# Written-out head groups without work for missing neighbours, and output additions ahead of the pair's second low part

## What is computed

```
# layer 0 (perceiver attention: keys of context and of the latents, RMS-normed q and k)
q  = rmsnorm(ln(x) @ Wq) * scale ;  k, v = split(concat(ln_x(ctx), ln(x)) @ Wkv) ; k = rmsnorm(k)
x += tanh(g) * (softmax(q @ k.T) @ v @ Wout + bout)
# layer 1 (keys of context and one null key)
x += tanh(g) * ln(softmax(q * scale @ k.T) @ v @ Wo)
```

## Time and profile before

| | |
|---|---|
| median of 3 runs | 4423.91 us (4422.67 to 4423.99) |
| the profiled execution | 4427.17 us |
| its span, first to last instruction | 4425.4 us |
| mean granted TensorE clock | 0.974 |
| TensorE busy | 4081.1 us, 92% |
| VectorE busy | 3433.7 us, 78% |
| ScalarE busy | 3199.6 us, 72% |
| GpSimd busy | 408.8 us, 9% |
| low parts, L824 | 1764 of 1223 ns |
| first attention layer | some 116 to 2294 us |
| second attention layer | some 2516 to 4367 us |

### The profile page before, as it was taken

The page is one execution under the profiler, slowest core; times in us unless marked ns, Lnnn a source line. Parts: engine busy times, 40 slices in busy tenths (PEclk is TensorE's granted clock), DMA queues, the critical chain, the costliest instruction groups (busy, mean ns, idle before and its releaser), DMA issues. The chain is left out here.

```text
span 4425.4 us, 74954 instructions
## 1 busy us (share of the span) xinstructions
PE 4081.1 (92%) x25901; PEld 2675.9 (60%) x26341; DVE 3433.7 (78%) x5288; ACT 3199.6 (72%) x5181; POOL 408.8 (9%) x348
## 2 busy tenths in 40 slices
PE   3999999999999999999978599999999999999995
PEld 2666666666666666666656366666666666666663
DVE  5888788787887878888867577777777777777775
ACT  3888888888878888888853367676766676666662
POOL 3111111111111111111110000000000000000000
PEclk9999999999999999999978699999999999999997
DMA  1000000000000000000003000000000000000001
GB/s 41 13 1 16 1 5 13 1 16 1 17 1 1 16 1 16 1 1 16 1 24 102 17 1 16 1 14 3 5 12 5 13 1 16 1 16 1 16 1 42
DMA packets 31247, 54.26 MB, mean 12 GB/s; under 512 B 9856, under 2 KB 19080, under 8 KB 28552
## 3 DMA queue, kind: packets, MB, share of 16 engines
q1 hardware_dynamic: 28808, 48.66, 3.5%
q10 hardware_dynamic: 2066, 0.69, 0.1%
HBM read 48.44 MB, written 0.88 MB: 11 GB/s over the span
## 5 line engine op out<-in xcount | busy, mean ns | idle before, releaser
L824 DVE TENSOR_TENSOR a_probs_lo<-a_probs 128x1024 fp32r<-128x1024 f32 x1764 | 2119.9, 1223 | 649.7 <-ACT a_probs L669 305.7
L665 ACT ACTIVATE a_probs<-scores_ps,a_c_bias,a_k_rstd 128x512 f32<-128x512 f32 x1892 | 1315.8, 775 | 31.6 <-PE scores_ps L1141 30.1
L1166 PE MATMUL out_ps<-a_probs_lo,a_v 128*128 128x512 f32 x3520 | 1135.6, 443 | 0.0
L1159 PE MATMUL out_ps<-a_probs,a_v 128*128 128x512 bf16 x3080 | 858.9, 390 | 113.6 <-issue 51.0
L669 ACT ACTIVATE a_probs<-scores_ps,a_c_bias 128x1024 f32<-128x1024 f32 x818 | 869.7, 1111 | 111.6 <-PE scores_ps L1141 110.7
L1141 PE MATMUL scores_ps<-a_q_hi,a_k_hi 64*128 64x512 f32 x3528 | 793.3, 445 | 11.0 <-ACT a_probs L665 6.3
L1166 PEld LDWEIGHTS out_ps<-a_probs_lo,a_v 128*128 128x128 f32 x3520 | 659.6, 188 | 220.8 <-issue 0.6
L1141 PE MATMUL scores_ps<-a_q_lo,a_k_hi 64*128 64x512 f32 x3528 | 702.8, 393 | 0.0
L1141 PE MATMUL scores_ps<-a_q_hi,a_k_lo 64*128 64x512 f32 x3528 | 698.4, 391 | 0.0
L1159 PEld LDWEIGHTS out_ps<-a_probs,a_v 128*128 128x128 f16 x3520 | 273.9, 97 | 592.8 <-issue 222.4
L634 ACT ACTIVATE a_v<-proj_ps 128x256 f16<-128x256 f32 x456 | 175.0, 384 | 520.7 <-PE proj_ps L1076 520.7
(11 more groups left out here) (233 smaller groups left out, 3455.8 us busy)
## 6 DMA issues: line engine op xcount, KB each, us to landing
a_den<-a_inv_row SPq DMA_DIRECT2D x18, 1024.0 KB, 4.7
normed<-in_L_xattn_we_g SPq DMA_DIRECT2D x18, 256.0 KB, 2.7
m_gate_spread<-m_combine_row SPq DMA_DIRECT2D x8, 512.0 KB, 4.1
a_wkv_raw<-in_L_xattn_wkv_g SPq DMA_DIRECT2D x18, 128.0 KB, 2.1
a_wo_raw<-in_L_xattn_wo_g SPq DMA_DIRECT2D x18, 128.0 KB, 2.0
m_w_raw<-in_L_ffn_w1T SPq DMA_DIRECT2D x8, 256.0 KB, 4.1
m_w_raw<-in_L_ffn_w2T SPq DMA_DIRECT2D x8, 256.0 KB, 4.5
m_gate_spread<-m_combine_row SPq DMA_DIRECT2D x8, 256.0 KB, 5.3
```

What stands on the lines that cost most here:

```text
L665: ins = nc.scalar.activation(probs[:, pb, e * 512:(e + 1) * 512], scores[:, b, e * 512:(e + 1) * 512], ACT.Exp, bias=cbias[:, tile:tile + ...
L824: nc.vector.tensor_tensor(plow[:, idx % NPL, :], probs[:, idx % NB, :], p_hi[:, idx % NB], ALU.subtract).then_inc(plo_ready, 1)
L1159: nc.tensor.matmul(outs[:, e * 512:(e + 1) * 512], v16[:, c % 2, t, e, :], p_hi[:, idx % NB, e * 512:(e + 1) * 512], start=t == 0, stop=False)
L1166: nc.tensor.matmul(outs[:, e * 512:(e + 1) * 512], v32[:, c % 2, t, e, :], plow[:, idx % NPL, e * 512:(e + 1) * 512], start=False, stop=t ...
```

## The change

1. The loops over groups are written out on all engines (`for g in range(NG)`), with constants in the waits. Group 0 leaves out the end of the group before it, and the last group the beginning of the one after: a new function `made(g, k)` tells if an item belongs to a group that exists. The last pair of the last group has no scores, exponentials or low parts of a next group. The counters of the waits are shifted by one group to match.
2. Where a unit ends, `add_out` stands ahead of the pair's second low part in every pair, not in crossed ones alone.
3. In a chunk of five tiles that is followed by one of three items (the fifth of the first layer, pairs 24 to 28) turns and loads have places given by a table `AMID`. Turn 15 goes from 24e to 24m, load 16 from 25m to 25s, turn 16 from 26m to 25e, load 17 from 27s to 26m, turn 17 from 28s to 27m.

The core of the diff:

```diff
+AMID = (0.55, 1.2, 2.0, 2.55, 3.55, 5.0)
...
             at = (k + 1) * pairs / (2 * n_items)
+            if pairs == 5 and n_items == 3:
+                at = AMID[k]
...
+        def made(g, k):
+            return g < NG - 1 or k < NI
...
                 def load_o(r):
-                    sp.wait_ge(ql_done, 2 * r + 2)
+                    if r < NG:
+                        sp.wait_ge(ql_done, 2 * r + 2)
+                    else:
+                        sp.wait_ge(f_add, 4 * (NG - 1))
...
# VectorE
-                with dve.Fori(0, NG // 4) as four:
-                    for sub in range(4):
-                        g = four * 4 + sub
-                        k0, s0 = g * NI, g * NS
-                        for i in range(NPR):
+                for g in range(NG):
+                    k0, s0 = g * NI, g * NS
+                    for i in range(NPR):
+                        more = g < NG - 1 or i < NPR - 1
+                        if more:
                             p_low(s0, 2 * i + 2)
-                            items(g, i, "s")
-                            if i in FINAL:
-                                f = FINAL.index(i)
-                                final_mul(g, f, side_no(g, "final", f))
-                            crossed = i in ENDS and ENDS[i][0][0] % 2 == 0
-                            if crossed:
-                                add_out(g, s0, *ENDS[i][0])
+                        items(g, i, "s")
+                        if i in FINAL and g:
+                            f = FINAL.index(i)
+                            final_mul(g, f, side_no(g, "final", f))
+                        if i in ENDS:
+                            add_out(g, s0, *ENDS[i][0])
+                        if more:
                             p_low(s0, 2 * i + 3)
-                            if i in ENDS and not crossed:
-                                add_out(g, s0, *ENDS[i][0])
+                        if g:
                             if i in FINAL:
                                 final_add(g, FINAL.index(i), side_no(g, "final", FINAL.index(i)))
...
+                        if g < NG - 1:
+                            query_work(g + 1, i)
+                        items(g, i, "me")
...
# TensorE
+                    for i in range(NPR):
+                        if g < NG - 1 or i < NPR - 1:
                             for k in range(2):
                                 score(s0, k0, g, 2 * i + 2 + k)
...
+                        if i in FINAL and g:
+                            final(g, FINAL.index(i), k0 + TURN[i - 1][1] + 1)
+                        if i in Q_ROW and g < NG - 1:
+                            project_q(g + 1, Q_ROW.index(i), k0 + TURN[i - 1][1] + 1)
+                        if i in Q_COL and g < NG - 1:
+                            transpose_q(g + 1, Q_COL.index(i), k0 + TURN[i - 1][1] + 1)
```

## The result

| | before | changed |
|---|---|---|
| median | 4423.52 us (4 runs) | 4355.68 us (4354.57 to 4355.8, 4 runs) |
| ratio to before | | 0.9846 [0.9829, 0.9863] |
| profiled execution | 4427.17 us | 4354.57 us |
| its span | 4425.4 us | 4352.7 us |
| mean granted TensorE clock | 0.974 | 0.976 |

The change took 67.8 us off the median; 4358 was forecast. (Rows 5 stand under a heading that names pairs 8 and 9; they are pairs 49 and 50 of the second group. The prices of their blocks are what they were said to be.)

The account below looks back on a forecast made before the run. TensorE's stream was taken to set the pace. Work taken out 37.5, loop 5.0, additions moved ahead 22.0 and new places 1 sum to 65.5 us, taken from the 4423.9 median: 4358 us, range 4337 to 4381.

Parts of the forecast that it names:

- Ordinary ends: Seven unit ends per first-layer group: additions ahead of the second low part remove 0.30 us each, 16.8 us in all.
- Group ends: Last unit end of a group: the longer wait for additions shrinks, 0.75 us seven times, 5.2 us; second layer 0.
- Work taken out: Work for groups that do not exist, at the first and last group, leaves TensorE's stream: 37.5 us with side effects.
- Loads and turns of the last chunk: Last group of each layer: three loads at 1.02 us and three transpose blocks at 0.54 go, 9.4 us in all.
- The loop: Jump back between groups, once per layer: writing groups out removes TensorE's idle time there, 5.0 us (4 to 6).
- Pairs 20 to 24: First layer, VectorE full with query work: a removed addition wait returns as a wait for the key's low part, 0.
- The new places: First-layer five-tile chunk, pairs 24 to 28: moved loads and transposes gain 0.2 us in seven groups, about 1 us.
- Queue blocking: Rival: moved additions hold the second low part in VectorE's in-order queue; 4472 us at 0.3 us per end; chance 0.04.
- order worth nothing: Rival: with additions moved ahead, TensorE meets the next late thing each time; 4380 us; chance 0.15.
- table worth 21: Rival, third listed: new places remove the crossing pair's wait and the half-clock stretch sometimes following it; 4337 us; chance 0.17.
- loop arithmetic: Rival: TensorE's waits without releaser come from loop arithmetic, so constants save up to 51 us; 4307 us; chance 0.03.
- missing work was partly hidden: Rival: half of the 37.5 us for work taken out was hidden; 4377 us; chance 0.08.

Follow-up runs that it names:

- kernel 7: Changed kernel with the crossed pair's additions also ahead of its first low part: 4338.54 us.
- Pad runs 5 and 6: Changed kernel with an unused VectorE sum between additions and second low part at uncrossed ends: over 512 columns 4380.98 us, over 1024 columns 4460.74 us.
- kernel 8: Changed kernel with the bound of the next group's queries behind the key's low part in pair 24: 4348.14 us.
- kernel 4: Changed kernel with the old places of loads and turns in the five-tile chunk: 4359.77 us.
- 1: Kernel before with only the new order of the additions, loops and missing work kept: 4395.25 us.
- 3: Changed kernel with the additions back behind the second low part, except in crossed pairs: 4386.21 us.
- kernel 9: Changed kernel with the crossed pair's additions ahead of its first low part and pair 24's query bound behind the key's low part: 4332.35 us.

## Why the prediction was right, and where it was not

**What bounds the kernel: right.** TensorE's stream sets the time. What was taken off TensorE's waits came off the time nearly in full (1.30 us of the 1.34 in kernel 7), with two exceptions in the query work of the first layer, where the order's gain came back as a loss one pair on (0.07 us in pair 21, 0.18 in pair 24).

**Ordinary ends: right in mechanism and size.** 0.30 was forecast and 0.27 to 0.29 measured, in the seven pairs named; the slack of the second low part was forecast at 0.65 and is 0.67. Pad runs 5 and 6 show that this slack is real and that it isn't the whole price: further consumers of VectorE's queue have less.

**Group ends: right in the first layer (0.74 of 0.75), wrong in the second.** The step that failed is the sentence that in the second layer "its waits are the crossing pair's, whose order stays". The earlier trace rows counts 30 waits and crossed pairs make 16. 5.0 us were missed, and with them the forecast that groups of the second layer keep their distance: it went from 228.6 to 227.8 us. In the first layer it fell from 268.9 to 265.9, the 3 that were forecast.

**Work taken out: mechanism right, one term mis-sized.** Projections, transposes and scores cost in the end what their rows said. Loads and turns of the last chunk gave 0.70 and 0.21 instead of 1.02 and 0.54. The changed kernel shows it in one group after another, low products with a turn, with a load and with neither in between, up to the scores:
```profile
1963.95 0.87 PEld L1181 LDWEIGHTS out_ps<-a_probs_lo,a_v 128*128 128x128 f32 x4
1964.87 0.37 PEld L1099 LDWEIGHTS proj_ps<-identity,normed 128*128 128x128 f32 x2
1965.41 0.19 PEld L1156 LDWEIGHTS scores_ps<-a_q_hi,a_k_hi 64*128 64x128 f32 x2 [0.17 <-issue]
...
1968.02 0.87 PEld L1181 LDWEIGHTS out_ps<-a_probs_lo,a_v 128*128 128x128 f32 x4
...
1969.96 0.19 PEld L1156 LDWEIGHTS scores_ps<-a_q_hi,a_k_hi 64*128 64x128 f32 x2
...
2208.50 0.88 PEld L1181 LDWEIGHTS out_ps<-a_probs_lo,a_v 128*128 128x128 f32 x4
2209.76 0.19 PEld L1156 LDWEIGHTS scores_ps<-a_q_hi,a_k_hi 64*128 64x128 f32 x2 [0.37 <-issue]
```
1.46 with a turn, 1.94 with a load, 1.26 with neither: 0.20 and 0.68. Scores directly behind low products show a gap of 0.37 that the block between them had covered. A block's price from start to start is what it costs to have it, not what its removal returns: the next block's gap has to be read from a place where the two stand side by side. The relief of VectorE was put at 3.0 and gave 1.9, inside its 1 to 4.

**The loop: the gap goes, its worth isn't shown.** Between the traces of before and changed the jumps make 6.0. In the trace of before both have a half-clock stretch; in its second trace the first layer's jump has none and the two pairs there are 1.5 shorter, but the two pairs behind them are 1.5 longer, so what the stretch cost isn't shown. The medians of two sets give 0 and 3.5. The forecast let unrolling cost nothing; group ends of the written-out kernel are 0.07 longer, 1.0 us in all. The Trainium skill, "Runtime: NRT & Kernel Launch", section on instruction fetch mechanics, has a taken branch out of the resident pages stall and straight code prefetched; the traces agree as to the gap, and no median here shows the gain.

**Pairs 20 to 24: nearly right.** The order gave 0.21 net in pairs 20 and 21 and 0 in 23 and 24, where 0 was forecast. The mechanism, a wait for the key's low part that takes over, is seen in pair 24, and kernel 8 removed it.

**The new places: right in size.** 1.0 was forecast, 0.1 a group and 0.85 in the last measured, with both rows as forecast: the load's wait (1.60) and the crossed pair's (1.71 to 1.34). The parts were not sized right: 1.1 was to be lost at the load, but with the old places it waits 1.09 for the same low part already (kernel 4), and 1.2 is gained in pairs 26 to 28 against 1.15 lost in 23 and 25.

**The base.** The sum was taken off the median, with 3.3 us between it and the profiled execution noted. 4.6 us of that execution's time are three half-clock stretches that the changed kernel doesn't have. The sum on the traces is 72.7, the medians differ by 67.8. Of the difference of 4.9, 3.6 is how far the profiled run of before lies above its median and 1.1 how far that of after lies below. On the traces the 65.5 lacks 5.0 (group ends), 4.6 (the stretches), 2.2 (places and pair 20), 1.0 (jumps) and 0.5 (tail), and has 3.9 (loads and turns), 1.1 (relief), 1.0 (ordinary ends) and 0.1 (transposes) too much. So the closeness of 4358 to 4355.7 is in part luck: misses of both signs, 13.3 and 6.1 us, and a base that held a disturbance.

**The rivals.** Queue blocking, order worth nothing, table worth 21, loop arithmetic: each is refuted by a kernel above (1; 1 and 3; 4) or by a row (the 59.0 us without releaser). One half of the third rival did come about, in that neither trace of the changed kernel has a half-clock stretch at the crossed pair, but kernel 4, without the table, has none in its one trace either. That the missing work was partly hidden holds for one term, with 3.9 us instead of 19.

## What to carry to other kernels

On an in-order engine, put the instruction that frees a buffer ahead of those whose results are wanted later, in every place of the pattern (28 us at the ends of units and groups here, 17 more in the crossed pair, 7.5 more for one key's low part), but first compute the slack of everything queued behind it: 0.6 us of delay cost nothing at the late unit ends and still 25 us in all. Look for a wait on the rows of weight loads too: those of the products showed 15 where the weight loads showed 80. Price removed work as the distance of its two neighbours with it less their distance without it. Count the waits of a line against the places of its pattern before calling a layer free of them.

## What the hardware showed that was not expected

- The granted clock of TensorE fell to the lower level in the midst of a stream, behind waits of 1.71 and 0.50 us with one small product between them: 13 times in 40 such places, not always in the same ones from one execution to the next, 1.5 us each. With a first wait of 1.38 or less it fell in none of 64, and in kernel 4, with 1.71 and 0.50 again, in none of 8.
- The mean granted clock of a profile was no measure of the kernel: it was 0.976 for the changed kernel and 0.968 for kernel 9, which is 23 us faster. The difference lies in the first 110 us, ahead of the first attention layer (0.99 and 0.70). Two runs of kernel 9 at 0.968 and 0.977 took 4332.34 and 4332.35 us.
- The same group end is 0.07 us longer in the kernel before with its loops written out: 5.04 us at all 14, against 4.97 at the 12 of the kernel before that have no jump. Why is open.
